# Sending the blank fill of the slot rows earlier in a DMA queue, in longer pieces

## The chip, the cores and the metric

The kernel is one program on one core of a Trainium2 chip. The core has a matrix engine (PE, TensorE), three engines for elementwise work (DVE, ACT, POOL) and SP, which here only issues DMA transfers. Sixteen DMA engines move data between the HBM and the on-chip memory of 128 partitions. The metric is the time of one execution in microseconds on the device, as the median of several runs.

## The reference

A small vision network in two layers over 32 images of 36 tokens (1152 tokens, 128 features), in float32:

```
h = patch_tokens(x)                                # stride-16 patches, four half-patch shifts, layernorm
h = h + transformer(layernorm(h))                  # rotary attention with 8 heads, relu feed-forward, two layernorms
h = h + gelu(layernorm(h) @ tril(W1).T + b1) @ tril(W2).T + b2
h = h + out(groupnorm((softmax(q1 k1) - lam * softmax(q2 k2)) v))     # lam from four vectors of 8 (lambdas)
h = h + moe(h)                                     # attention, then a router: top 2 of 64 experts
# in moe:
pos  = number of earlier picks of the same expert;  keep = pos < 72
buf  = zeros(64, 72, 128);  buf[expert, pos] = token          # 4608 slot rows
y    = gelu(buf @ w1 + b1) @ w2 + b2                          # 64 experts, 512 hidden
out  = x + sum over the two picks of gate * y[expert, pos]
```

Most of the 4608 slots are named by a token; those that are not must hold zeros and an invalid token number.

## The kernel before

All stages up to the router work on four parts of 288 tokens (8 images each), numbered 0 to 3. Each stage name with its part, such as `tok_z:3`, stands in one list per engine (`ORDERS_FOUND`), and the engine executes its list in that order; semaphores join the lists. The start of the lists, as far as it matters here: PE runs `tok_z:0 tok_shift:0 tok_z:1 tok_turn:0 tok_shift:1 tok_z:2 tok_turn:1 tok_shift:2 tok_z:3 tok_turn:2 src_turn:0 tok_shift:3 rope_qk:0`, with filler matmuls (128x128 on the weights, results unused) between some of them; DVE runs `tok_shift:0 tok_norm_a:0 tok_shift:1 tok_norm_a:1 src_norm_a:0 tok_shift:2`; ACT runs `tok_norm_b:1 tok_turn:2 src_norm_b:0` behind POOL's reciprocal root for the same norms. `tok_z` multiplies the patches of a part (waits for `x_in[b]`); `tok_norm_a` takes the moments of a part. In the code of DVE the stage `tok_norm_a:1` begins with `dve.wait_ge(S["lambdas_in"], 16)` and two small products of the lambdas.

SP issues the loads in the order of its code: the patch weights, patches of part 0, columns, constants, patches 1, the rows of biases, patches 2, the other weights (`wT`, blocks 6 and up), patches 3, `lambdas`, router, b1, b2, and the first 11 of the 64 experts' weights (`ring`). All of these go into one queue of SP.

The slot rows (`xslot`, in the HBM, named slot_rows in the profile, 4608 rows of 130 floats) must be filled with a blank row before the tokens are scattered into them: 128 zeros, a token number out of bounds (`NOWHERE`) and one more zero. POOL writes this blank row with two memsets at the very start into the first 130 columns of `hid`, on all 128 partitions, and signals `blank_made`. The fill is one DMA of SP, at the end of its first batch. Two places wait for its end (`blank_sent`): ACT in `net_in:0`, which is the first to write into `hid`, and POOL in `rt_count:0`, ahead of the first scatter (an indirect DMA from `xrow`). After the scatter SP reads the slot rows back for the experts.

Later, POOL clears `mid` and stores it twice into expert_rows, another tensor in the HBM, with one piece per partition. Past the router the kernel walks through the 64 experts, whose weights come through a ring of 11 buffers.

Of the kernel before, what the change touches and what calls it, by code (L numbers as in the profile page):

```python
# [28 lines left out]
D = 128  # L29
# [19 lines left out]
CAP = 2 * (T * 2 // E)  # L49
SLOTS = E * CAP  # L50
ST = SLOTS // D
XW = D + 2
RING = 11
CHUNKS = (2, 6, 8, 8, 8, 8, 8, 8, 8)
# [9 lines left out]
NOWHERE = 1.0e6  # L64
# [208 lines left out]
def build(nc, ins, out):  # L273
# [46 lines left out]
    with ctx:  # L320
        def sb(name, shape, dt=F32):
            return ctx.enter_context(nc.sbuf_tensor(name, shape, dt))

        def sem(name):
            return ctx.enter_context(nc.semaphore(name))
# [47 lines left out]
        third = Share()  # L373
        xrows = third.take([E, XW])
        xe = third.take([NX, CAP])
# [23 lines left out]
        hid = sb("hid", [D, FC, 2, TB])  # L399
# [24 lines left out]
        kept_gate = sb("kept_gate", [TP, NT, 2])  # L424

        xrow = sb("xrow", [TP, 2, TPB, 2, XW])
        blank = hid[:, 0, 0, 0:XW]
        gm = sb("gm", [TP, NT, E])
        put_u = sb("put_u", [CAP, E], U32)

        xslot = nc.dram_tensor("slot_rows", [SLOTS, XW], F32, kind="Internal").ap()
        ytok = nc.dram_tensor("expert_rows", [2 * T, D], F32, kind="Internal").ap()
# [9 lines left out]
        S = {n: sem(n) for n in names}  # L442
# [80 lines left out]
        def tiles(t, b):  # L523
            return t[:, TPB * b:TPB * b + TPB, :]
# [8 lines left out]
        def back_of(b):  # L533

            return ring[0:TP, b, 0:TPB * 2 * D].rearrange("p (n c) -> p n c", n=TPB)
# [4 lines left out]
        @block.sync  # L540
        def _(sp):

            sp.dma_start(wT[:, 0:6, :], ins["weights"][:, 0:6, :]).then_inc(S["patch_weights_in"], 16)
            sp.dma_start(patchT[:, 0, 0:3, :], ins["patches"][:, 0, 0:3, :]).then_inc(S["first_patches_in"], 16)
            sp.dma_start(patchT[:, 0, 3:6, :], ins["patches"][:, 0, 3:6, :]).then_inc(x_in[0], 16)
            sp.dma_start(cols[:, :], ins["cols"]).then_inc(S["cols_in"], 16)
            sp.dma_start(cst[:, :], ins["const"]).then_inc(S["const_in"], 16)
            for b in range(1, NB):
                sp.dma_start(patchT[:, b, :, :], ins["patches"][:, b, :, :]).then_inc(x_in[b], 16)
                if b == 1:  # L550
                    sp.dma_start(rows[:, :, :], ins["rows"].partition_broadcast(TP).rearrange("p (n c) -> p n c", c=D)).then_inc(S["rows_in"], 16)
                if b == 2:
                    sp.dma_start(wT[:, 6:NBLOCKS, :], ins["weights"][:, 6:NBLOCKS, :]).then_inc(S["weights_in"], 16)
            sp.dma_start(lambdas[:, :, :], ins["lambdas"].partition_broadcast(SROWS).rearrange("p (n h) -> p n h", h=H)
                         ).then_inc(S["lambdas_in"], 16)
            sp.dma_start(wr[:, :], ins["router"]).then_inc(S["late_in"], 16)
            sp.dma_start(b1T[:, :, :], ins["b1"]).then_inc(S["late_in"], 16)
            sp.dma_start(b2nat[:, :], ins["b2"]).then_inc(S["late_in"], 16)
            for e in range(RING):
                sp.dma_start(ring[:, e, :], ins["experts"][e]).then_inc(w_here[e], 16)  # L560
            sp.wait_ge(S["blank_made"], 1)
            sp.dma_start(xslot.rearrange("(p n) c -> p n c", p=D), blank[:, :].unsqueeze(1).broadcast_to([D, ST, XW])
                         ).then_inc(S["blank_sent"], 16)
            for b in range(NB - 1):
                sp.wait_ge(slots_sent[b], 16 * 2 * TPB)
            for n in range(2 * TPB):
                sp.wait_ge(last_sent[n], 16)
            for c in range(len(CHUNKS)):
                at = slice(chunk_at[c], chunk_at[c + 1])
                sp.dma_start(xrows[0:CAP, at, :], xslot.rearrange("(s e) c -> s e c", e=E)[:, at, :]).then_inc(rows_here[c], 16)  # L570
            for e in range(RING, E):
                s = e % RING
                sp.wait_ge(S["ys_ready"], e - RING + 1)
                sp.dma_start(ring[:, s, :], ins["experts"][e]).then_inc(w_here[s], 16)

            sp.wait_ge(S["ys_ready"], E)
            for i in range(NY):
                sp.wait_ge(ys_gone[i], 16 * (E // NY))
            for b in range(NB):
                sp.dma_start(back_of(b).rearrange("p n c -> p (n c)"), ytok.rearrange("(b p m) c -> b p (m c)", b=NB, p=TP)[b]  # L580
                             ).then_inc(back_in[b], 16)
            for b in range(NB):
                sp.wait_ge(S["final_ready"], b + 1)
                sp.dma_start(out.rearrange("i s c -> (i s) c").rearrange("(n p) c -> p n c", p=TP)[:, TPB * b:TPB * b + TPB, :],
                             tiles(res, b)).then_inc(S["stored"], 16)
            sp.wait_ge(S["stored"], 16 * NB)
# [3 lines left out]
        def _(pool):  # L590
            st = Steps(pool, S["pool_step"])

            st.step(pool.memset(minus_half[:, :], -0.5))
            st.link(pool.memset(blank[:, :], 0.0))
            pool.memset(blank[:, D:D + 1], NOWHERE).then_inc(S["blank_made"], 1)
            st.step(pool.memset(xTp[:, :, :, :], 0.0))
            pool.memset(run[:, 0, :], 0.0).then_inc(S["run_ready"], 1)
            st.step(pool.memset(ones16[:, :], 1.0))
# [24 lines left out]
            for stage, b in ORDER["pool"]:  # L623
# [52 lines left out]
                if stage == "rt_count":  # L676

                    t = slice(TPB * b, TPB * b + TPB)
# [786 lines left out]
```

## Time and profile before

| | |
|---|---|
| median of 3 runs | 389.16 us (387.92 to 389.21) |
| the profiled execution | 389.98 us, its span 388.3 us |
| PE busy | 347.7 us (90%) |
| DVE, ACT, POOL busy | 233.7, 220.9, 197.4 us |
| DMA | 21239 packets, 50.20 MB |
| the fill, issue to landing | 30.2 us |

PE's busy share is high partly because of the filler matmuls, so it does not say that PE is what sets the end at each place. The DMA engines are full in the first 50 us and again in the expert stage, and nearly idle between them. For a change of the first stage the rows of that stage count.

### The profile page before, as it was taken

To read this page: it belongs to the slowest core of one execution; us is meant where nothing else is said; L and a number is where in the kernel's file an instruction comes from. 1 tells how busy PE (TensorE), PEld (TensorE's weight loads), DVE (VectorE), ACT (ScalarE), POOL (GpSimd) and SP (SyncE) were. 2 spreads that over 40 slices of the span, in tenths; PEclk is the share of its full clock that TensorE was granted. 3 is DMA by queue.
4 is the path that set the end of the run, shared out by engine and by line. 5 is a ranking of instruction groups with operands and counts; after the bars stand their busy time and mean duration, and the time that the engine had idled before them with its cause. 6 is when DMAs were issued, how large, how long until landed. Compare 5 with 4: busy or idle time off the path is not lost.

```text
span 388.3 us, 11371 instructions
## 1 busy us (share of the span) xinstructions
PE 347.7 (90%) x4424; PEld 315.2 (81%) x4424; DVE 233.7 (60%) x615; ACT 220.9 (57%) x640; POOL 197.4 (51%) x312
## 2 busy tenths in 40 slices
PE   8969799999988999997899899499999999999950
PEld 8748687887866889696778788399999999999950
DVE  1446788763489899897868985623335433333314
ACT  1247677777659876677488563103555555555520
POOL 3169687587841112236345767720555555555550
PEclk9999999999999999998999999559999999999995
DMA  7999924000000000000000100037899989999206
GB/s 277 374 391 334 150 28 125 2 2 1 2 3 0 3 3 2 3 2 3 3 3 2 33 9 13 15 95 202 272 320 316 322 308 316 327 324 314 85 9 182
DMA packets 21239, 50.20 MB, mean 129 GB/s; under 512 B 4116, under 2 KB 10340, under 8 KB 21058
## 3 DMA queue, kind: packets, MB, share of 16 engines
q1 hardware_dynamic: 18146, 46.96, 37.9%
q0 software_dynamic: 3040, 2.52, 2.4%
q8 instruction: 36, 0.59, 0.6%
q14 instruction: 17, 0.14, 0.1%
HBM read 43.97 MB, written 7.72 MB: 133 GB/s over the span
## 4 chain that ended last, share of the span: by engine, by line
PE 57%; DVE 12%; ACT 11%; POOL 9%; DMA 6%; issue 4%; SPq 1%; POOLq 0%; DVEq 0%
PE bank L728 34%; PE scores L728 18%; DMA lambdas<-in_lambdas 4%; ACT work L1037 4%; PE bank L803 3%; ACT norm L1037 3%; POOL rstd L613 3%; DVE mx L1266 2%; DVE stats L1203 2%; DVE work L1275 1%; ACT src L1037 1%; PE bank L979 1%; POOL rstd L611 1%; ACT xrow L1037 1%; POOL norm L664 1%
## 5 line engine op out<-in xcount | busy, mean ns | idle before, releaser
L1037 ACT ACTIVATE work<-scores,b1T 128x72 f32<-128x72 f32 x256 | 61.3, 322 | 66.9 <-PE scores L728 66.9
L728 PE MATMUL bank<-ring,work 128*72 128x128 f32 x512 | 97.3, 274 | 0.0
L720 POOL DMA_INDIRECT expert_rows<-work,put_u x64 | 59.9, 935 | 61.7 <-issue 37.7
L728 PE MATMUL scores<-work,ring 128*128 128x72 f32 x512 | 89.0, 258 | 0.2 <-ACT work L1037 0.2
L728 PEld LDWEIGHTS scores<-work,ring 128*128 128x128 f32 x512 | 76.9, 191 | 0.3 <-issue 0.3
L728 PE MATMUL bank<-wT 128*128 128x128 f32 x504 | 72.3, 283 | 2.7 <-ACT work L1037 2.7
L728 PEld LDWEIGHTS bank<-wT 128*128 128x128 f32 x504 | 63.8, 193 | 5.7 <-ACT work L1037 3.1
L1037 ACT ACTIVATE work<-bank 128x288 f32<-128x288 f32 (+3 forms) x136 | 46.7, 376 | 34.4 <-PE bank L728 27.0
L1437 DVE TENSOR_SCALAR work<-bank,work 72x128 f32<-72x128 f32 x64 | 22.2, 347 | 67.5 <-PE bank L728 67.5
L728 PEld LDWEIGHTS bank<-ring,work 128*72 128x72 f32 x512 | 53.8, 145 | 0.2 <-ACT work L1037 0.2
L611 POOL TENSOR_SCALAR rstd<-mv 96x3 f32<-96x3 f32 x32 | 10.1, 315 | 54.8 <-DVE mv L1206 53.6
L613 POOL TENSOR_TENSOR rstd<-rstd,minus_half 96x3 f32<-96x3 f32 x32 | 28.2, 882 | 2.7
L690 POOL DMA_INDIRECT slot_rows<-xrow,flat_u x24 | 24.0, 1001 | 10.5 <-issue 6.1
L1408 DVE TENSOR_SCALAR work<-bank,cols 128x72 f32<-128x72 f32 x64 | 21.7, 341 | 6.8 <-PE bank L979 6.8
L728 PE MATMUL bank<-xTp,wT 128*128 128x288 f32 x80 | 22.9, 416 | 2.3 <-ACT work L1037 1.4
L1037 ACT ACTIVATE work<-work 100x1152 f32<-100x1152 f32 (+1 forms) x20 | 20.2, 1016 | 8.3 <-DVE work L1275 7.0
L1266 DVE TENSOR_REDUCE mx<-scores 100x32 f32<-100x1152 f32 x16 | 21.6, 1351 | 5.0 <-PE scores L728 4.9
L728 PE MATMUL bank<-wT,xTp 128*128 128x128 f32 x192 | 23.8, 277 | 0.4 <-DVE work L1252 0.4
L728 PEld LDWEIGHTS bank<-wT,xTp 128*128 128x128 f32 x192 | 22.5, 192 | 1.4 <-issue 1.2
L1284 DVE TENSOR_REDUCE sm<-work 100x32 f32<-100x1152 f32 x16 | 21.4, 1340 | 3.5 <-ACT work L1037 3.3
L1299 DVE TENSOR_TENSOR work<-work,sm 100x1152 f32<-100x1152 f32 x16 | 21.8, 1360 | 0.6
L1275 DVE TENSOR_TENSOR work<-scores,mx 100x1152 f32<-100x1152 f32 x16 | 21.7, 1358 | 0.6
(159 smaller groups left out, 594.2 us busy)
## 6 DMA issues: line engine op xcount, KB each, us to landing
ring<-in_experts SPq DMA_DIRECT2D x64, 512.0 KB, 5.0
work<-in_patches SPq DMA_DIRECT2D x3, 864.0 KB, 10.6
slot_rows<-hid SPq DMA_DIRECT2D x1, 2340.0 KB, 30.2
work<-slot_rows SPq DMA_DIRECT2D x7, 292.5 KB
wT<-in_weights SPq DMA_DIRECT2D x1, 1664.0 KB, 13.9
expert_rows<-mid POOLq DMA_DIRECT2D x2, 576.0 KB, 5.1
ring<-expert_rows SPq DMA_DIRECT2D x4, 288.0 KB, 4.0
expert_rows<-work,put_u POOLq DMA_INDIRECT x64, 4.4
```

The costliest lines, as they stand in the source:

```text
L611: st.step(pool.tensor_scalar(n, m, -1.0, None, ALU.mult))
L613: st.link(pool.tensor_tensor(r, r, minus_half[0:TP, 0:TPB], ALU.pow))
L690: pool.indirect_dma_start(out=xslot[:, :], out_offset=bass.IndirectOffsetOnAxis(ap=flat_u[:, TPB * b + n, k:k + 1], axis=0), in_=xrow[:, b ...
L720: pool.indirect_dma_start(out=ytok[:, :], out_offset=bass.IndirectOffsetOnAxis(ap=put_u[:, e:e + 1], axis=0), in_=ys[0:CAP, e % NY, :], in ...
L728: return nc.tensor.matmul(o, a, b, start=start, stop=stop)
L1037: return nc.scalar.activation(o, i, f, **kw)
L1266: st.link(v.tensor_reduce(m3, sc, AX_X, ALU.max))
L1275: v.tensor_tensor(e4, sc, m3.unsqueeze(3).broadcast_to([SROWS, QUADS, 2 * PAIRS, SEQ]), ALU.subtract).then_inc(S["exp_in"], 1)
L1284: st.link(v.tensor_reduce(s3, e4, AX_X, ALU.add))
L1299: v.tensor_tensor(to, e4, s3.unsqueeze(3).broadcast_to([SROWS, QUADS, 2 * PAIRS, SEQ]), ALU.mult).then_inc(S["map_scaled" if stage[:3] == ...
L1408: v.tensor_scalar(xe[:, e % NX, :], banks[i][:, 0:CAP], col("L1_ffn_ln2_g"), col("L1_ffn_ln2_b"), ALU.mult, ALU.add).then_inc(S["xe_ready" ...
L1437: v.tensor_scalar(ys[0:CAP, f % NY, :], banks[f % 2][0:CAP, 0:D], xrows[0:CAP, f, D + 1:D + 2], None, ALU.mult).then_inc(S["ys_ready"], 1)
```

## The change

Three edits. The blank source becomes 12 blank rows side by side in `hid` (1560 columns, with `NOWHERE` in 12 of them). The fill writes the same 4608 rows from it, as 384 pieces of 12 rows, where it wrote 4608 pieces of one row. And its issue, with the wait for `blank_made`, moves up in SP's code: behind the second load of `wT`, ahead of the patches of part 3.

```diff
+BLANKS = 12
...
-        blank = hid[:, 0, 0, 0:XW]
+        blank = hid[:, :, :, :].rearrange("p c a t -> p (c a t)")[:, 0:BLANKS * XW].rearrange("p (n c) -> p n c", c=XW)
...
                 if b == 2:
                     sp.dma_start(wT[:, 6:NBLOCKS, :], ins["weights"][:, 6:NBLOCKS, :]).then_inc(S["weights_in"], 16)
+                    sp.wait_ge(S["blank_made"], 1)
+                    sp.dma_start(xslot.rearrange("(p k n) c -> p k (n c)", p=D, n=BLANKS),
+                                 blank.rearrange("p n c -> p (n c)").unsqueeze(1).broadcast_to([D, ST // BLANKS, BLANKS * XW])
+                                 ).then_inc(S["blank_sent"], 16)
...
             for e in range(RING):
                 sp.dma_start(ring[:, e, :], ins["experts"][e]).then_inc(w_here[e], 16)
-            sp.wait_ge(S["blank_made"], 1)
-            sp.dma_start(xslot.rearrange("(p n) c -> p n c", p=D), blank[:, :].unsqueeze(1).broadcast_to([D, ST, XW])
-                         ).then_inc(S["blank_sent"], 16)
...
-            st.link(pool.memset(blank[:, :], 0.0))
-            pool.memset(blank[:, D:D + 1], NOWHERE).then_inc(S["blank_made"], 1)
+            st.link(pool.memset(blank[:, :, :], 0.0))
+            pool.memset(blank[:, :, D], NOWHERE).then_inc(S["blank_made"], 1)
```

SP's instructions from the constants on, before the change (in_patches are the patches of parts 1, 2 and 3, in_b is b1 and then b2, slot_rows<-hid is the fill):

```order
L549 DMA work<-in_patches 128x1728
L551 DMA rows<-in_rows 96x1408
L549 DMA work<-in_patches 128x1728
L553 DMA wT<-in_weights 128x3328
L549 DMA work<-in_patches 128x1728
L554 DMA lambdas<-in_lambdas 100x32
L556 DMA wr<-in_router 128x64
L557 DMA b1T<-in_b 128x256
L558 DMA b2nat<-in_b 64x128
L560 DMA ring<-in_experts 128x1024 x11
L562 DMA slot_rows<-hid 4608x1x130 [waits blank_made]
```

And the same stretch of SP after it:

```order
L550 DMA work<-in_patches 128x1728
L552 DMA rows<-in_rows 96x1408
L550 DMA work<-in_patches 128x1728
L554 DMA wT<-in_weights 128x3328
L556 DMA slot_rows<-hid 384x1x1560 [waits blank_made]
L550 DMA work<-in_patches 128x1728
L559 DMA lambdas<-in_lambdas 100x32
L561 DMA wr<-in_router 128x64
L562 DMA b1T<-in_b 128x256
L563 DMA b2nat<-in_b 64x128
L565 DMA ring<-in_experts 128x1024 x11
```

The fill went past 11 expert loads, b2, b1, the router, the lambdas and the third batch of patches; nothing else on SP changed its place.

The start of POOL's program after the change (minus_half is a constant, hid holds the blank rows):

```order
L595 MEMSET minus_half 128x3
L596 MEMSET hid 128x1560
L597 MEMSET hid 128x12 [waits pool_step]
L598 MEMSET xTp 128x1152
L599 MEMSET run 96x64
L600 MEMSET ones 96x96
L601 MEMSET work 128x2048
L603 CAST before<-cst 96x96 [waits const_in]
```

The order is that of before; the two memsets of hid were 128x130 and 128x1.

## Rows read from the trace of the kernel before

**Rows 1.** The page: the span, and the DMA queue of the instructions.
```profile
span 388.3 us, 11371 instructions
...
q8 instruction: 36, 0.59, 0.6%
```

**Rows 2.** Chain that ended last, 0 to 80 us: start us, us, what.
```profile
6.21 16.35 DMA lambdas<-in_lambdas
...
29.68 7.33 PE bank L728 x52
...
45.23 1.82 issue
```

**Rows 3.** Table of waits: engine, line, releaser, us in total, times, longest.
```profile
DVE lambdas L1221 <- DMA lambdas<-in_lambdas: 4.2, 1, 4.2
```

**Rows 4.** Timeline of PE: start us, us, operation, idle time before it.
```profile
21.31 0.38 PE L728 MATMUL bank<-wT 128*128 128x128 f32 x2
22.38 3.18 PE L728 MATMUL bank<-work,wT 128*128 128x288 f32 x12 [0.69 <-DMA work<-in_patches]
...
26.52 0.90 PE L728 MATMUL bank<-cst,work 128*96 128x128 f32 x6 [0.74 <-DVE work L1235]
```

**Rows 5.** Timeline of SP's issues.
```profile
5.18 0.44 SPq L553 DMA_DIRECT2D wT<-in_weights  x1
5.66 0.51 SPq L549 DMA_DIRECT2D work<-in_patches  x1
...
22.73 1.15 SPq L562 DMA_DIRECT2D slot_rows<-hid  x1
```

**Rows 6.** DMA issues: KB each, median us from issue to landing.
```profile
slot_rows<-hid SPq DMA_DIRECT2D x1, 2340.0 KB, 30.2
...
wT<-in_weights SPq DMA_DIRECT2D x1, 1664.0 KB, 13.9
expert_rows<-mid POOLq DMA_DIRECT2D x2, 576.0 KB, 5.1
```

**Rows 7.** Windows: busy time of each engine, then granted clock, DMA share, GB/s.
```profile
58.50:62.50 4.00, 3.59 (x81) 2.92 (x80) 3.90 (x6) 3.38 (x10) 2.10 (x6) 1.00 0.91 269
22.50:34.50 12.00, 10.11 (x61) 8.23 (x61) 8.83 (x38) 6.30 (x17) 9.23 (x20) 1.00 1.03 410
36.50:49.50 13.00, 10.75 (x191) 9.17 (x190) 10.13 (x17) 8.28 (x23) 9.69 (x20) 1.00 1.22 151
```

**Rows 8.** Timelines of POOL at the start, and of ACT at net_in:0.
```profile
0.83 0.21 POOL L594 MEMSET hid<- 128x130 f32 x1
...
1.13 1.06 POOL L596 MEMSET xTp<- 128x1152 f32 x1
...
8.41 0.26 POOL L601 CAST before<-cst 96x96 bf16<-96x96 f32 x1 [4.27 <-DMA cst<-in_const]
...
64.58 1.66 ACT L1037 ACTIVATE hid<-bank,cols 128x288 f32<-128x288 f32 x4
```

**Rows 9.** PE's timeline and windows at 242 to 262 us, columns as above.
```profile
245.23 0.29 PE L728 MATMUL bank<-oh_both,before 96*96 96x64 bf16 x1 [2.88 <-DVE oh_both L1364]
...
256.79 7.16 PE L728 MATMUL scores<-wT 128*128 128x128 f32 x44
...
243.50:244.00 0.50, 0.00 (x0) 0.00 (x0) 0.50 (x5) 0.48 (x2) 0.23 (x1) 0.92 0.00 0
244.00:244.50 0.50, 0.00 (x0) 0.00 (x0) 0.43 (x3) 0.50 (x1) 0.47 (x1) 0.50 0.17 44
...
260.50:261.00 0.50, 0.50 (x4) 0.50 (x3) 0.00 (x0) 0.00 (x0) 0.00 (x0) 0.52 0.78 200
261.00:261.50 0.50, 0.50 (x7) 0.50 (x6) 0.00 (x0) 0.00 (x0) 0.00 (x0) 1.00 0.72 183
```

**Rows 10.** Timeline of PE's weight loads, at two breaks inside groups of 64.
```profile
47.05 0.17 PEld L728 LDWEIGHTS scores<-work 32*36 32x36 f32 x11 [2.00 <-issue]
...
148.10 0.18 PEld L728 LDWEIGHTS scores<-work 32*36 32x36 f32 x13 [0.30 <-issue]
```

## The prediction

> **What bounds the kernel now.** I read the page first: the span of the profiled execution is 388.3 us [rows 1]. Since the change touches only the first fifty microseconds, I then read the chain that ended last, in order of time. Its first long piece is not computation: from 6.21 us on the chain hangs on one transfer, that of the lambdas, for 16.35 us, and then on PE, in an almost unbroken line of TensorE, ACT and DVE work [rows 2]. The table of waits says who stands there: DVE waits 4.2 us for the lambdas [rows 3]. They are a small transfer (100 x 32 numbers) and nobody needs them before the second attention layer, but the code puts their product ahead of tok_norm_a:1 on DVE, so the whole program passes through them. The second thing that arrives at that moment is the last batch of patches: PE ends the filler ahead of tok_z:3 at 21.69 us, waits, and starts tok_z:3 at 22.38 us [rows 4]. Lambdas and patches land within 0.3 us of each other because they follow one another in one queue.
>
> That queue is SP's. It issues the big weight block at 5.18 us, the last patches at 5.66 us, and the fill of the slot rows only at 22.73 us, behind the eleven expert loads [rows 5]. The weights land 13.9 us after their issue, at about 19.1 us; the fill takes 30.2 us and lands at 52.9 us [rows 6]. Between 22.5 and 34.5 us the sixteen DMA engines move 410 GB/s at a share of 1.03, so they are full; while the fill runs, from 36.5 to 49.5 us, they are full too (1.22) but move only 151 GB/s [rows 7].
>
> **The change part by part.**
>
> The rows of the fill. Before: 4608 pieces of 520 bytes, 2,396,160 bytes, about 15.9 us at 151 GB/s. After: 384 pieces of 6240 bytes. The trace has no store of that kind on SP's queue. From above in speed: loads on this queue run at 410 GB/s [rows 7], which makes 5.8 us. From below: the two stores of expert_rows from mid, 576 KB from 96 partitions, so 6144 bytes a piece [rows 6], ran at 269 GB/s with a share of 0.91 [rows 7]; full engines would make 269 / 0.91 = 296 GB/s of it, which gives 8.1 us. One row has the queue, the other the direction and the piece size, and neither has both, so I take the middle, **7.0 us**, and keep 5.8 and 8.1.
>
> The Trainium skill, "DMA: Bandwidth & Descriptors", Specifications, puts a core's share of the HBM at about 358 GB/s and the fabric at 435 GB/s; an estimate from the page is 6.7 us or 5.5 us for the fill. The trace's 410 GB/s on loads lies above the first figure, so for a core alone I do not hold the kernel to it.
>
> The place of the fill. It now stands in SP's queue ahead of the last patches and the lambdas. Everything of SP behind it goes later by its length: patches 3, lambdas, router, b1, b2, eleven expert loads. Router, b1, b2 and the experts are used in the router and expert stages, long after all of this, so they pay nothing. The weights stand ahead and pay nothing. The last patches hold PE at tok_z:3, the lambdas hold DVE at tok_norm_a:1, and neither has any slack today: both engines were already idle when they came [rows 3, 4]. I looked for work that could fill the longer wait: on DVE everything behind tok_norm_a:1 is in order (src_norm_a:0, tok_shift:2), ACT needs POOL's result of it, and PE needs the patches. So start of both: later by **7.0 us**. SP's wait for blank_made costs nothing: the memset grows from 130 to 1560 columns, by 1152 columns in 1.06 us about 1.4 us instead of 0.21, and ends near 2.5 us, before SP comes there at about 5.7; POOL idles 4.27 us for the constants afterwards [rows 8], which covers the 1.2 us more. Were that cover gone, it would be 1.2 us.
>
> TensorE's clock. PE would now idle from 21.69 to about 29.4 us, 7.7 us. In the trace PE stops at 242.35 us and starts again at 245.23; the granted clock is 0.92 in the half microsecond before 244, and 0.50 after it [rows 9]. So a shorter gap than the new one took the clock to 1.2 GHz. It came back at 261.0 us, 4.2 us after the dense run of 44 matmuls began at 256.79 [rows 9]. tok_z:3 is such a dense run (3.18 us [rows 4]). At half speed for 4.2 us it loses 2.1 us, of which 0.74 us is PE's own idle time ahead of tok_turn:2 [rows 4], where it waits for DVE: **1.4 us** on the path. Floor 0 (no fall). Ceiling: the clock stays low as long as it did after 245.23, 15.8 us, and all of it is PE work: 7.9 less 0.74, or 7.2 us. I take the value near the floor since the work that follows (the 7.33 us run of PE on the chain at 29.68 [rows 2]) is full-width and dense.
>
> The stall inside the fill. In the middle of the 64 score matmuls of rope_scores:1, which wait for nothing among themselves, PE stands still for 1.82 us at 45.23, and that is on the chain [rows 2]; the weight loads show the same hole, 2.00 us, while a hole of the same place in a later group, with DMA idle, is 0.30 us [rows 10]. The page shows a queue for instructions with 36 packets of 0.59 MB in all [rows 1]. My reading, an inference, is that the next instructions came late behind the fill's 520-byte rows. After the change the fill is over by 27 us and the expert loads by about 43 us, and this group runs near 52 us, so the hole should shrink to its size without DMA: 1.82 less 0.30, **1.5 us** won. Bounds 0 and 1.8.
>
> The Trainium skill, "Runtime: NRT & Kernel Launch", Instruction fetch mechanics, says that instructions come in 16 KiB blocks over a DMA queue and that this is mostly hidden. The 36 packets agree with the size. If the hole had another cause, as "mostly hidden" would suggest, the sum would be 1.5 us longer.
>
> The end of the fill. It lands at 52.9 us before, and ACT's first write to hid, which waits for it, starts at 64.58 us [rows 6, 8]; the scatter that also waits for it comes in the router stage. Finishing it earlier wins nothing. Behind 30 us nothing else hangs on a fixed arrival; the chain runs engine to engine, so what is lost at 22 us is not given back.
>
> Sum: 7.0 + 1.4 - 1.5 = **+6.9 us**. The profiled execution has 389.98 us (span 388.3 and 1.7 around it), so 396.9; it lies 0.8 us above the median of 389.16, so the median after is **396.0**.
>
> **The rivals.** (1) The clock stays at half for long after the gap, as between 245 and 261 us: up to 7.2 instead of 1.4 us, 401.9. Against: the work there was small matmuls until 256.79. (2) The fill does not get faster, because its rate is that of scattered writes to memory and not of pieces: 15.9 us instead of 7.0, 405. Against: the stores from mid at 269 GB/s. (3) Not slower: loads use one direction of each engine and the fill the other, so that fill and last patches pass side by side. The decision point is the arrival of the last patches: up to 25.8 us (22.38 and 3.4, of which 1.5 are won back and 1.9 can't be told) it is no measurable change; fully side by side it is 389.2 - 1.5 = 387.7. For it: the share of DMA goes over 1 during the fill. Against: the pieces of one queue are taken in order, as the lambdas behind the patches show. The Trainium skill, "DMA: Bandwidth & Descriptors", Queues, rings and completion order, has it that descriptors are consumed in ring order on each engine but may finish out of order, which leaves both open.
>
> **How the numbers follow.** Forecast 0.80; clock long 0.07; fill slow 0.05; side by side 0.08. The terms' bounds give 5.8 + 0 - 1.8 = 4.0 and 8.1 + 7.2 - 0 = 15.3; all at their worst together is unlikely, so the range goes from 392.5 (just under the low sum, 393.2) to 401.0. What a measurement of this kernel tells from no change is about 0.5%, 1.9 us. Slower 0.92; of the side by side case 0.05 falls within and 0.03 under.
>
> **What would show it.** Last patches: tok_z:3 starts at 28.2 to 30.5 us instead of 22.38, and DVE's wait for the lambdas grows from 4.2 to about 11 us. DMA at some 300 to 400 GB/s throughout 19 to 43 us and idle after. PEclk below 1 for some 6 us after 23 us. The hole in rope_scores:1 under 0.5 us. From the first rope map to the end, the same distances as before. I would be wrong if tok_z:3 starts before 26 us, or if the later stages draw together.

## The result

| | before | changed |
|---|---|---|
| median of 4 runs | 389.19 us (387.92 to 390.31) | 396.22 us (395.78 to 396.61) |
| profiled execution, its span | 389.98, 388.3 us | 395.92, 394.2 us |

The ratio is 1.0182 (95% interval 1.0146 to 1.0218): the change makes the kernel 1.8% slower. Medians in this document are over all executions of a kernel, while ratios and their intervals leave out the executions that took over 1.5% longer than the fastest of the same kernel. The forecast was 396.0 us in a range of 392.5 to 401.0. The path on which the time is lost is the one forecast; several sizes on it are not, and they partly cancel.

The timeline of PE in the changed kernel, which answers to [rows 4]:

```profile
21.05 0.39 PE L730 MATMUL bank<-wT 128*128 128x128 f32 x2
28.20 4.78 PE L730 MATMUL bank<-work,wT 128*128 128x288 f32 x12 [6.76 <-DMA work<-in_patches]
...
33.21 0.90 PE L730 MATMUL bank<-cst,work 128*96 128x128 f32 x6
```

tok_z:3 starts 5.82 us later (28.20 against 22.38), PE idles 6.76 us ahead of it instead of 0.69, and it takes 4.78 us instead of 3.18. tok_turn:2 starts 6.69 us later (33.21 against 26.52).

The waits of its first 60 us, where [rows 3] had 4.2 us:

```profile
DVE lambdas L1223 <- DMA lambdas<-in_lambdas: 11.1, 1, 11.1
...
PE bank L730 <- DMA work<-in_patches: 7.3, 2, 6.8
```

Both waits have grown by about the length of the fill, PE's by 6.1 us and DVE's by 6.9 us. The fill itself, in the table of DMA issues that answers to [rows 6]:

```profile
slot_rows<-hid SPq DMA_DIRECT2D x1, 2340.0 KB, 19.7
...
wT<-in_weights SPq DMA_DIRECT2D x1, 1664.0 KB, 14.1
```

SP issued the fill at 5.55 us and the weights at 5.05, so they landed at 25.3 and 19.2 us: the fill took 6.1 us of the queue. The windows of the changed kernel (busy time of PE, PEld, DVE, ACT, POOL, then granted clock, DMA share, GB/s), which answer to [rows 7, 9]:

```profile
22.00:24.00 2.00, 0.00 (x0) 0.00 (x0) 0.00 (x0) 0.00 (x0) 0.00 (x0) 1.00 1.01 412
24.00:26.00 2.00, 0.00 (x0) 0.00 (x0) 0.00 (x0) 0.00 (x0) 0.00 (x0) 0.66 1.00 394
26.00:28.00 2.00, 0.00 (x0) 0.00 (x0) 0.00 (x0) 0.00 (x0) 0.00 (x0) 0.50 0.80 284
...
31.00:31.50 0.50, 0.50 (x2) 0.36 (x2) 0.44 (x4) 0.00 (x0) 0.42 (x2) 0.53 1.04 418
31.50:32.00 0.50, 0.50 (x3) 0.39 (x3) 0.48 (x2) 0.00 (x0) 0.50 (x1) 1.00 1.07 426
...
164.00:165.00 1.00, 1.00 (x7) 0.83 (x7) 0.14 (x1) 0.00 (x0) 0.00 (x0) 0.80 0.00 0
...
167.00:168.00 1.00, 1.00 (x9) 1.00 (x8) 0.96 (x2) 0.41 (x1) 1.00 (x1) 0.50 0.03 8
168.00:169.00 1.00, 1.00 (x13) 1.00 (x12) 1.00 (x3) 0.95 (x3) 0.55 (x2) 1.00 0.00 0
```

The reader is to see four things. From 22 to 28 us none of the four computing engines does anything. The long pieces go to the HBM at 412 GB/s, as fast as the loads. The clock falls to 1.2 GHz (0.50) from 24.5 us on, while PE waits, and is back at 2.4 GHz in the half microsecond after 31.5. And it falls once more from 164 to 168 us, where nothing of the change is near. The kernel before comes to the same instructions 4 us earlier and has 1.00 there:

```profile
160.00:161.00 1.00, 1.00 (x9) 0.81 (x8) 0.17 (x1) 0.00 (x0) 0.00 (x0) 1.00 0.00 0
```

Going down the two timelines at the same instruction gives the difference in start, before to changed: tok_turn:2 26.52 to 33.21 (+6.7), the first flip of probabilities on PE 50.73 to 55.00 (+4.3), the scores behind it in the second attention 158.16 to 162.13 (+4.0), the group norm's product 177.85 to 183.26 (+5.4), the end of the span +5.9. So the profile loses 6.7 us, wins 2.4 by 55 us, and loses 1.4 again at the dip of the clock. The remaining 0.5 us comes in small steps behind. These 5.9 us are the difference of the two profiled executions. The medians differ by 7.0 us, since the profiled execution of before took 0.8 us more than its median and that of the changed kernel 0.3 us less. Much of the 0.8 us seems to lie in the first stage: three later traces, with the long pieces at the old place, have the same transfers in the same order up to tok_z:3, and start it at 21.34, 21.39 and 21.45 us, not at 22.38. What made the loads land later in the one trace of the kernel before is open. Against these traces the delay of the first stage is 6.8 us at tok_z:3 and 7.4 us at tok_turn:2.

### The profile page after: what moved, and what is told of

The parts are those of the page before. It is cut to its first block, busy times and chain, and to the rows that moved or that the text cites. A ratio compares the mean times of both kernels' runs of the same rounds, so it can differ in the third digit from the quotient of the medians.

```text
span 394.2 us, 11371 instructions
## 1 busy us (share of the span) xinstructions
PE 350.4 (89%) x4424; PEld 317.4 (81%) x4424; DVE 233.6 (59%) x615; ACT 220.8 (56%) x640; POOL 197.6 (50%) x312
## 4 chain that ended last, share of the span: by engine, by line
PE 61%; ACT 10%; DVE 9%; POOL 8%; DMA 7%; issue 3%; SPq 1%; POOLq 0%; DVEq 0%
PE bank L730 38%; PE scores L730 17%; DMA work<-in_patches 6%; ACT work L1039 4%; PE bank L805 3%; ACT norm L1039 3%; POOL rstd L615 2%; ACT src L1039 1%; PE bank L981 1%; DVE stats L1205 1%; POOL rstd L614 1%; PE bank L739 1%; DMA ring<-expert_rows 1%; POOL norm L666 1%; POOL norm L665 1%
## 5 line engine op out<-in xcount | busy, mean ns | idle before, releaser
L613 POOL TENSOR_SCALAR rstd<-mv 96x3 f32<-96x3 f32 x32 | 9.0, 282 | 63.6 <-DVE mv L1208 62.4
L615 POOL TENSOR_TENSOR rstd<-rstd,minus_half 96x3 f32<-96x3 f32 x32 | 28.2, 881 | 2.7
L1410 DVE TENSOR_SCALAR work<-bank,cols 128x72 f32<-128x72 f32 x64 | 21.7, 341 | 7.0 <-PE bank L981 7.0
L1301 DVE TENSOR_TENSOR work<-work,sm 100x1152 f32<-100x1152 f32 x16 | 21.7, 1359 | 0.6
L1277 DVE TENSOR_TENSOR work<-scores,mx 100x1152 f32<-100x1152 f32 x16 | 21.7, 1357 | 0.6
```

What stands on the lines that cost most here:

```text
L615: st.link(pool.tensor_tensor(r, r, minus_half[0:TP, 0:TPB], ALU.pow))
L1277: v.tensor_tensor(e4, sc, m3.unsqueeze(3).broadcast_to([SROWS, QUADS, 2 * PAIRS, SEQ]), ALU.subtract).then_inc(S["exp_in"], 1)
L1301: v.tensor_tensor(to, e4, s3.unsqueeze(3).broadcast_to([SROWS, QUADS, 2 * PAIRS, SEQ]), ALU.mult).then_inc(S["map_scaled" if stage[:3] == ...
L1410: v.tensor_scalar(xe[:, e % NX, :], banks[i][:, 0:CAP], col("L1_ffn_ln2_g"), col("L1_ffn_ln2_b"), ALU.mult, ALU.add).then_inc(S["xe_ready" ...
```

## The experiments

The first four ran on one chip (the kernel before: 389.33 us median there), the other seven on chips where the kernel before takes 402 us. There the first 200 us of the long pieces at the old place run as on the first chip, and from about 216 us on, in the last stages ahead of the router and in the router, holes appear in ACT and PE whose releaser the profile does not name. What makes them is open. They begin far behind the first stage, so for those runs the early part of the timelines carries more than the totals.

**The place alone.** The kernel before, with its fill of 4608 short pieces moved to the new place.

```diff
                 if b == 2:
                     sp.dma_start(wT[:, 6:NBLOCKS, :], ins["weights"][:, 6:NBLOCKS, :]).then_inc(S["weights_in"], 16)
+                    sp.wait_ge(S["blank_made"], 1)
+                    sp.dma_start(xslot.rearrange("(p n) c -> p n c", p=D), blank[:, :].unsqueeze(1).broadcast_to([D, ST, XW])
+                                 ).then_inc(S["blank_sent"], 16)
...
-            sp.wait_ge(S["blank_made"], 1)
-            sp.dma_start(xslot.rearrange("(p n) c -> p n c", p=D), blank[:, :].unsqueeze(1).broadcast_to([D, ST, XW])
-                         ).then_inc(S["blank_sent"], 16)
```

> The fill keeps its 4608 pieces of 520 bytes and only moves ahead of the last patches. If the delay is the length of the fill in the queue, it is 15.9 us here (2.4 MB at the 151 GB/s of the kernel before), so tok_z:3 starts near 38 us; with the 2.4 us that the rest of the first stage won in the changed kernel and the clock about level, the time is 389 + 15.9 - 2.4 = 403 us, at least 401. Rival: the pieces' size does not matter to what waits behind, then it is 396 as with long pieces. Second rival: the loads behind pass it by, then 387 to 390.

Measured: 406.41 us, ratio 1.0454 (1.0382 to 1.0526). PE's timeline:

```profile
39.14 5.97 PE L728 MATMUL bank<-work,wT 128*128 128x288 f32 x12 [17.07 <-DMA work<-in_patches]
```

tok_z:3 starts 16.8 us later than before, close to the 15.9 us worked out, and runs wholly at the low clock (5.97 us against 3.18). Those two differences, 0.9 and 2.8 us less PE's slack of 0.7, make 3.0 of the 3.4 us by which the time lies over the 403 expected. The delay follows the length of the fill in the queue; both rivals fall. SP's timeline shows more:

```profile
5.60 0.65 SPq L555 DMA_DIRECT2D slot_rows<-hid  x1
6.29 19.56 SPq L549 DMA_DIRECT2D work<-in_patches  x1
25.90 1.16 SPq L557 DMA_DIRECT2D lambdas<-in_lambdas  x1
```

SP itself hangs 19.56 us in the issue of the patches behind the 4608 pieces; with 384 pieces that issue takes 0.64 us. So at the new place the long pieces are worth 10 us: 17.1 us are lost without them and 7.0 us with them.

**The long pieces alone**, at the old place behind the expert loads. The cut is shown against the kernel before; the 12 blank rows in hid are those of the change.

```diff
             for e in range(RING):
                 sp.dma_start(ring[:, e, :], ins["experts"][e]).then_inc(w_here[e], 16)
             sp.wait_ge(S["blank_made"], 1)
-            sp.dma_start(xslot.rearrange("(p n) c -> p n c", p=D), blank[:, :].unsqueeze(1).broadcast_to([D, ST, XW])
+            sp.dma_start(xslot.rearrange("(p k n) c -> p k (n c)", p=D, n=BLANKS),
+                         blank.rearrange("p n c -> p (n c)").unsqueeze(1).broadcast_to([D, ST // BLANKS, BLANKS * XW])
                          ).then_inc(S["blank_sent"], 16)
```

> The fill in pieces of 12 rows, at its old place behind the expert loads. It should run from 36 to 42 us and land near 42.5 instead of 52.9. If the hole of 1.8 us inside the score matmuls of rope_scores:1 came from the 520-byte pieces, it is gone and flip:0 starts 2.1 to 2.4 us earlier: 386.8 to 387.1. Rival: the hole has nothing to do with the fill, then 389.2. Nothing in it should move the start of tok_z:3 (22.4 us).

Measured: 387.34 us, ratio 0.9951 (0.9916 to 0.9985). PE's timeline:

```profile
21.45 3.16 PE L730 MATMUL bank<-work,wT 128*128 128x288 f32 x12
...
25.80 0.90 PE L730 MATMUL bank<-cst,work 128*96 128x128 f32 x6 [0.97 <-DVE work L1237]
...
47.59 1.57 PE L805 MATMUL bank<-cst,work 100*128 100x100 f32 x16
```

The first flip starts 3.1 us earlier than in the profile of before, but only 2.4 us of that are the fill's: tok_turn:2 was 0.7 us early already, before the fill had begun, and tok_z:3 0.9 us, which the expectation had not allowed for. Its weight loads on PE, to be read against [rows 10]:

```profile
43.34 0.74 PEld L730 LDWEIGHTS scores<-work 32*36 32x36 f32 x64 [0.15 <-issue]
```

The 64 loads of rope_scores:1 are one row, with no hole. The fetch of instructions gives a likely reason. In the kernel before a block of instructions arrives in the microsecond from 43, while the fill's short pieces are in flight:

```profile
q1 hardware_dynamic: 281, 0.15, 116.6%
q8 instruction: 1, 0.02, 8.9%
```

In the kernel with long pieces that block arrives in the microsecond from 39, 4 us earlier, although the queues are as full:

```profile
q1 hardware_dynamic: 63, 0.39, 98.0%
q8 instruction: 1, 0.02, 7.0%
```

The columns are packets, MB, and the time of the packets as a share of the sixteen engines. Less the 1.1 us by which this execution runs ahead there, the block is about 3 us earlier. The profile does not say for which engine a block is, so that the hole of [rows 2] is this block coming late remains an inference; that the hole goes with the short pieces is shown.

This run also separates the two parts of the change. The changed kernel differs from it by the place alone: 396.22 against 387.34 us, 8.9 us (387.34 is from the first chip, where the kernel before took 389.33 us). The long pieces at the old place win 2.0 us.

**The lambdas ahead of the fill**, the last patches behind it.

```diff
                     sp.dma_start(wT[:, 6:NBLOCKS, :], ins["weights"][:, 6:NBLOCKS, :]).then_inc(S["weights_in"], 16)
+                    sp.dma_start(lambdas[:, :, :], ins["lambdas"].partition_broadcast(SROWS).rearrange("p (n h) -> p n h", h=H)
+                                 ).then_inc(S["lambdas_in"], 16)
                     sp.wait_ge(S["blank_made"], 1)
...
-            sp.dma_start(lambdas[:, :, :], ins["lambdas"].partition_broadcast(SROWS).rearrange("p (n h) -> p n h", h=H)
-                         ).then_inc(S["lambdas_in"], 16)
```

> The changed kernel with the lambdas ahead of the fill; the last patches stay behind it. If the patches alone hold the path, DVE goes on at about 20.5 us, tok_z:3 still starts at 28.2 and ends near 33.2 at the low clock, and the time stays at 396.2 (395.5 to 396.5). Rival: the wait for the lambdas is what costs, then tok_turn:2 comes near 27 us and the time is about 388 to 390.

Measured: 394.97 us, ratio 1.0167 (1.0097 to 1.0237).

```profile
27.84 5.12 PE L730 MATMUL bank<-work,wT 128*128 128x288 f32 x12 [6.64 <-DMA work<-in_patches]
32.80 0.38 PE L730 MATMUL bank<-wT 128*128 128x128 f32 x2
33.02 0.82 PE L730 MATMUL bank<-cst,work 128*96 128x128 f32 x6
```

DVE is free from 18.85 us, and tok_turn:2 still starts at 33.0. The patches and the slow clock by themselves cost the whole delay. The median lies 1.2 us under that of the changed kernel, but four executions between 392.86 and 396.89 us do not settle such a difference. The profiled one is the fastest of them. It is 3.1 us shorter than that of the changed kernel, 0.4 us of it by 40 us; the rest comes at two dips of the clock of the changed kernel that it does not have, from 164 and from 188 us (the kernel before has the second one, from 182 us, too).

**The last patches ahead of the fill**, the lambdas behind it.

```diff
                     sp.dma_start(wT[:, 6:NBLOCKS, :], ins["weights"][:, 6:NBLOCKS, :]).then_inc(S["weights_in"], 16)
-                    sp.wait_ge(S["blank_made"], 1)
-                    sp.dma_start(xslot.rearrange("(p k n) c -> p k (n c)", p=D, n=BLANKS),
-                                 blank.rearrange("p n c -> p (n c)").unsqueeze(1).broadcast_to([D, ST // BLANKS, BLANKS * XW])
-                                 ).then_inc(S["blank_sent"], 16)
+            sp.wait_ge(S["blank_made"], 1)
+            sp.dma_start(xslot.rearrange("(p k n) c -> p k (n c)", p=D, n=BLANKS),
+                         blank.rearrange("p n c -> p (n c)").unsqueeze(1).broadcast_to([D, ST // BLANKS, BLANKS * XW])
+                         ).then_inc(S["blank_sent"], 16)
             sp.dma_start(lambdas[:, :, :], ins["lambdas"].partition_broadcast(SROWS).rearrange("p (n h) -> p n h", h=H)
                          ).then_inc(S["lambdas_in"], 16)
```

> The changed kernel with the last patches ahead of the fill; the lambdas alone stay behind it. If the lambdas by themselves hold the path as long as the patches do, DVE waits to 29 us, tok_turn:2 starts at 33 and the time is 396. The clock may fall once more, since PE then idles from 25.8 to 33 us, which would add up to 0.8. Rival: the patches are what costs, then 388 to 390.

Measured: 396.40 us, ratio 1.0202 (1.0123 to 1.0281).

```profile
21.88 3.12 PE L730 MATMUL bank<-work,wT 128*128 128x288 f32 x12
...
33.08 1.59 PE L730 MATMUL bank<-cst,work 128*96 128x128 f32 x6 [7.85 <-DVE work L1237]
```

tok_z:3 runs at once, and tok_turn:2 still starts at 33.1, since DVE waits for the lambdas (10.4 us). It is 1.59 us long instead of 0.90 because now it is the one that meets the low clock. The low clock then leaves PE 0.75 us behind the changed kernel at src_turn:0 (36.95 against 36.20 us), as the expectation allowed. So either of the two transfers alone costs the full delay, and moving one of them back wins nothing in the stage where it waits.

**The clock, in two runs**: 27 filler matmuls instead of one ahead of tok_z:3, with the lambdas as in the changed kernel, and with the lambdas ahead of the fill.

```diff
-    tok_z:0=5 tok_shift:0=4 tok_shift:1=1 tok_turn:1=2 tok_z:3=1 tok_turn:2=1 src_turn:0=3 rope_qk:0=4 tok_turn:3=2
+    tok_z:0=5 tok_shift:0=4 tok_shift:1=1 tok_turn:1=2 tok_z:3=27 tok_turn:2=1 src_turn:0=3 rope_qk:0=4 tok_turn:3=2
```

> The changed kernel with 27 filler matmuls instead of 1 ahead of tok_z:3, so that PE works through most of its wait (0.25 us each, to about 27.7 us) and the clock stays at 2.4 GHz. If the low clock after the wait costs the path nothing because DVE, held by the lambdas until 29.3 us, is as late as PE, tok_z:3 takes 3.2 instead of 4.8 us, tok_turn:2 still starts at 33.2 us and the early stages stand where they stood. The prediction's term says otherwise: 1.4 us won, tok_turn:2 near 32. The later dip of the clock at 164 us may come or not, 1.4 us; the total 394.5 to 396.5.

> The lambdas ahead of the fill and the 27 filler matmuls together. With the lambdas alone moved, PE's tok_z:3 at the low clock (5.1 us) holds tok_turn:2 at 33.0 us. If the clock is what costs there, both together start it at about 31.2 us, 1.8 us earlier, and the time is 1.8 us under that of the kernel with the lambdas moved, 393.2. Rival: something else holds tok_turn:2 and it stays at 33.

Measured: 407.76 us, ratio 1.0197 (1.0151 to 1.0244), and 404.80 us, ratio 1.0118 (1.0093 to 1.0144). The filler with the lambdas behind the fill:

```profile
28.51 3.18 PE L730 MATMUL bank<-work,wT 128*128 128x288 f32 x12 [1.18 <-DMA work<-in_patches]
31.52 0.38 PE L730 MATMUL bank<-wT 128*128 128x128 f32 x2
34.11 0.90 PE L730 MATMUL bank<-cst,work 128*96 128x128 f32 x6 [2.20 <-DVE work L1237]
```

and with the lambdas ahead:

```profile
28.21 3.18 PE L730 MATMUL bank<-work,wT 128*128 128x288 f32 x12 [0.40 <-DMA work<-in_patches]
31.22 0.38 PE L730 MATMUL bank<-wT 128*128 128x128 f32 x2
31.44 0.82 PE L730 MATMUL bank<-cst,work 128*96 128x128 f32 x6
```

In both, tok_z:3 takes 3.18 us again, so the 1.6 us (1.9 us with the lambdas ahead) were the clock's. In the first they win nothing: PE merely waits 2.20 us for DVE, and tok_turn:2 starts at 34.11 us, 0.9 us later than expected, since in this execution the lambdas came 0.9 us later (30.18 us). In the second, tok_turn:2 starts at 31.44 instead of 33.02, 1.6 us won of the 1.8 expected. The low clock costs the changed kernel nothing by itself; it costs 1.6 us only once the lambdas are out of the way.

**Long traffic of long pieces**: the long pieces at the old place, and three more such stores to a tensor that nothing reads (its declaration is left out here, as are the two waits for `blank_sent`, which now count all four stores).

```diff
+            for i in range(3):
+                sp.dma_start(spare.rearrange("(i p k n) c -> i p k (n c)", i=4, p=D, n=BLANKS)[i],
+                             blank.rearrange("p n c -> p (n c)").unsqueeze(1).broadcast_to([D, ST // BLANKS, BLANKS * XW])
+                             ).then_inc(S["blank_sent"], 16)
```

> The long pieces at the old place, and behind them three more stores of the same size and piece length into another tensor of the HBM, which nothing reads, so that the DMA engines are full with long pieces until about 60 us. ACT's write to hid waits for all four. If the hole in rope_scores:1 needs short pieces, it is absent here too (weight loads idle under 0.5 us inside the group) and the time stays near 387.3, or a little over for net_in:0. Rival: any full queue delays it, then the hole of about 2 us is back at 43 us and the time is 389 or more.

Measured: 405.90 us, ratio 1.0106 (1.0046 to 1.0166). Its profiled execution was the longest of its four (409.68 us), so only its first 65 us are read here. The stores run at the loads' rate:

```profile
42.00:58.00 16.00, 13.95 (x303) 12.32 (x305) 12.77 (x26) 12.57 (x35) 13.29 (x20) 1.00 1.02 412
```

And the weight loads:

```profile
43.30 0.74 PEld L735 LDWEIGHTS scores<-work 32*36 32x36 f32 x64 [0.16 <-issue]
...
53.38 0.63 PEld L735 LDWEIGHTS bank<-wT,xTp 128*128 128x128 f32 x5 [1.64 <-issue]
61.66 0.60 PEld L735 LDWEIGHTS bank<-work 128*32 128x32 f32 x33 [3.46 <-issue]
```

Both expectations were half right. The hole in rope_scores:1 stays away, but two others open at 53.4 and 61.7 us, inside groups that wait for nothing. The next two blocks of instructions arrive in the microseconds from 50 and from 59:

```profile
q1 hardware_dynamic: 65, 0.41, 101.1%
q8 instruction: 1, 0.02, 6.8%
...
q0 software_dynamic: 68, 0.36, 95.0%
q8 instruction: 1, 0.02, 6.6%
```

With long pieces alone, where the queues are idle, they arrive from 44 and 52 us. At the second block it is POOL's own stores (queue 0) that fill the engines. So blocks come late behind long pieces too, and short pieces are not needed for a hole, as far as one execution can show it. What long pieces seem to have done for the kernel is to end the traffic before the next block was wanted.

**Better orders.** Three runs beside each other: long pieces alone again; with the lambdas moved up behind the columns; and with, on top of that, the last patches ahead of the big weight block and the fill behind it (this last one also ran a first time in the set before).

```diff
             sp.dma_start(cols[:, :], ins["cols"]).then_inc(S["cols_in"], 16)
+            sp.dma_start(lambdas[:, :, :], ins["lambdas"].partition_broadcast(SROWS).rearrange("p (n h) -> p n h", h=H)
+                         ).then_inc(S["lambdas_in"], 16)
...
-                if b == 2:
-                    sp.dma_start(wT[:, 6:NBLOCKS, :], ins["weights"][:, 6:NBLOCKS, :]).then_inc(S["weights_in"], 16)
...
-            sp.dma_start(lambdas[:, :, :], ins["lambdas"].partition_broadcast(SROWS).rearrange("p (n h) -> p n h", h=H)
-                         ).then_inc(S["lambdas_in"], 16)
+            sp.dma_start(wT[:, 6:NBLOCKS, :], ins["weights"][:, 6:NBLOCKS, :]).then_inc(S["weights_in"], 16)
+            sp.wait_ge(S["blank_made"], 1)
+            sp.dma_start(xslot.rearrange("(p k n) c -> p k (n c)", p=D, n=BLANKS),
+                         blank.rearrange("p n c -> p (n c)").unsqueeze(1).broadcast_to([D, ST // BLANKS, BLANKS * XW])
+                         ).then_inc(S["blank_sent"], 16)
             sp.dma_start(wr[:, :], ins["router"]).then_inc(S["late_in"], 16)
```

> The kernel with long pieces at the old place, once more, beside the next two on one chip. Theory: 0.5 to 0.8% faster than the kernel before (2.4 to 3 us), since the hole in rope_scores:1 is gone. Rival: the 0.5% seen first was chance, then it is the same within 0.3%.

> Long pieces at the old place and the lambdas moved up, behind the columns. DVE then works on tok_norm_a:1 from about 20 us. If the lambdas were 1 us of the path (PE waited 0.97 us for DVE ahead of tok_turn:2), tok_turn:2 starts near 24.9 us instead of 25.8 and the time is 0.7 to 1 us under that of long pieces alone. Rival: it is not, PE's own work or the patches hold it, then the same.

> Long pieces, in another order: the lambdas behind the columns, the last patches ahead of the big weight block, then the weights, the fill, router, b1, b2, experts. Nothing that the first stages wait for stands behind the fill. tok_z:3 should start right behind its filler at 21.7 us, and tok_turn:2 at about 25.2 us instead of the 25.8 of the kernel with long pieces alone: 386.5 us, 0.6 to 1 us under that. Rival: the weights, now last, hold rope_qk:0 (they would have to come after 29 us), then it is slower than long pieces alone.

> Long pieces, the lambdas behind the columns, the last patches ahead of the big weight block and the fill behind it, once more beside the others. If the patches of part 3 still set the path with the lambdas early, it is up to 0.7 us under the kernel with the lambdas moved; if PE reaches tok_z:3 no earlier than they land in any case, it is the same. It should be 0.8 to 1.2% faster than the kernel before.

Measured: long pieces alone 399.00 us, ratio 0.9911 (0.9873 to 0.9949); with the lambdas up 401.72 us, 0.9990 (0.9952 to 1.0028); the full new order 401.04 us, 0.9990 (0.9951 to 1.0029), and again 399.91 us, 0.9991 (0.9951 to 1.0032). Long pieces alone beat the kernel before on the first chip. On this one the sign is the same, but it is less sure than the interval says: the executions of either kernel scatter over 10 us, and the medians of all of them are 399.00 and 401.99 us. The other orders do not clear the noise of this chip. PE's timeline with the lambdas up:

```profile
21.95 0.38 PE L730 MATMUL bank<-wT 128*128 128x128 f32 x2
22.31 3.18 PE L730 MATMUL bank<-work,wT 128*128 128x288 f32 x12
25.32 0.38 PE L730 MATMUL bank<-wT 128*128 128x128 f32 x2
25.54 0.88 PE L730 MATMUL bank<-cst,work 128*96 128x128 f32 x6
```

PE no longer waits for DVE, but its filler ahead of tok_z:3 starts at 21.95 us where it starts at 21.10 with long pieces alone on the same chip, presumably since every load behind the lambdas comes later, the constants and the patches of part 1 among them. tok_turn:2 is at 25.54 against 25.68: of the 0.94 us that PE idled there, 0.14 is left as gain. With the full new order tok_z:3 starts at 22.45 and 22.21 us where 21.7 was expected, and tok_turn:2 at 25.81 and 25.56 where 25.2 was. So all three expectations of a further gain were wrong, the 0.8 to 1.2% under the kernel before among them. Nor does the first stage explain that the kernel with the lambdas up has a median 2.7 us above that of long pieces alone: its profiled execution is 0.8 us ahead at 255 us and falls behind only from 259 us on, in the router stage, at a hole of 2.58 us that has no named releaser.

## Why the prediction was right, and where it was not

**The path.** Right: last patches and lambdas stand behind the fill and both come later by about its length. The place alone (+16.8 us at tok_z:3 for a fill of 15.9) and the two runs with one of them moved back (33.0 and 33.1 us at tok_turn:2) show it. With long pieces the place costs 8.9 us by the medians (7.0 + 1.4 = 8.4 were put down, but the 8.9 hold the dip of the clock at 164 us, which was not foreseen), and the pieces win 2.0 us (1.5 were put down).

**The length of the fill, 7.0 us.** Too high for the fill itself: it took 6.1 us of the queue, near the 5.8 us of the fast bound, with long pieces at 412 GB/s. The delay of the patches is less sure. It is 5.82 us against the one profile of the kernel before, and 6.8 us against the long pieces at the old place, close to the 7.0; behind the fill the queue moved only 284 GB/s from 26 to 28 us, and why it did is open. The row of the stores from mid (296 GB/s when scaled to full engines [rows 7]), on which I leaned for the middle, is of a short transfer from POOL's queue, presumably with its start and end in the window. The 358 GB/s that the Trainium skill, "DMA: Bandwidth & Descriptors", Specifications, gives as a core's share of the HBM is passed here by stores as well as loads, on this one core. Against the profile of before the lambdas came 6.68 us later, 0.86 more than the patches ahead of them; what delays them that much more I did not isolate.

**The clock, 1.4 us.** It fell and came back as described, after 3.3 us of tok_z:3 and not 4.2, and tok_z:3 lost 1.6 us by it, 0.9 more than PE's 0.74 us of slack. But as a term added to the fill's length it was wrong: that sum took both branches to be held equally long, which leaves the slack of PE against DVE as it was, while DVE was held for 6.68 us by the lambdas and PE for 5.82 by the patches. The two branches met at 33.2 us, PE's 5.82 + 1.60 - 0.74 = 6.68 and DVE's 6.68. Filler matmuls alone won nothing at tok_turn:2; with the lambdas ahead they won 1.6 us. Fill and clock together were put at 8.4 us; at tok_turn:2 they measured 6.7 us against the profile of before, or 7.4 us against the long pieces at the old place.

**The hole, 1.5 us won.** Right in kind, too small: by the first flip 2.4 us were won. Of these, 0.3 us came ahead of the hole, where PE had waited 0.42 us for DVE at 41.50 us, and 2.1 us at the hole itself. PE's hole went to 0, not to the 0.30 us of the row I compared it with, and DVE had been idle 1.97 us behind it. That the fetch of instructions is the cause was an inference; the block that comes about 3 us earlier bears it out and does not prove it. By the Trainium skill, "Runtime: NRT & Kernel Launch", Instruction fetch mechanics, the fetch is mostly hidden. The traces agree for idle queues; with full ones the block from 39 us cost nothing, and the later ones of the run with three more stores stand beside holes of up to 3.46 us.

**Not given back.** The statement that nothing behind 30 us gives the time back held, but the reverse was missed: a new dip of the clock at 164 us costs 1.4 us in the profiled execution; why it comes there is open. By the steps, 6.9 us was 7.0 + 1.4 - 1.5, and the profiles give 6.7 - 2.4 + 1.4 + 0.2 = 5.9. The median's 396.22 lies so near to 396.0 partly by chance: the medians are 7.0 us apart, 1.1 more than the profiled executions, and an overrated clock, an underrated hole and a dip that nobody foresaw about cancel.

**The rivals.** The clock staying low for long did not happen (7 us after 24.5). The fill as slow as before fell with its 6.1 us. Side by side fell with the arrival of the patches at 28.2 us.

## What to carry to other kernels

A transfer that nobody waits for belongs behind all that somebody waits for in its queue; its price when it stands ahead is its bytes over the rate of the queue, paid once on each branch that waits, and branches that wait in parallel do not add. Before adding a clock penalty to a wait, follow the other branch to the point where they meet. Long pieces are worth having wherever the transfer stands: here they won 2 us at the harmless place and 10 us at the harmful one. And one profiled execution is one execution: before reading a difference of 1 us out of two traces, compare each with the median of its set.

## What the runs showed of the hardware

Pieces of 520 bytes from the on-chip memory to the HBM moved at 151 GB/s, pieces of 6240 bytes at 412 GB/s in the same queue. Behind 4608 short pieces SP's own issue of the next load took 19.56 us; behind 384 long ones it took 0.64 us.

The granted clock of the same instructions was not the same in every kernel. In the changed kernel it was 0.50 between about 164 and 168 us, where the kernel before ran the same instructions at 1.00, 4 us earlier; it is not seen there with the lambdas ahead of the fill, nor with the last patches ahead. The dip from 188 us of the changed kernel stands in the profile of before too, 6 us earlier, and is absent with the lambdas ahead. Each is read from one execution. The first of them moved the total by about 1.4 us, more than some of the edits compared here.

Blocks of 16 KiB of instructions (0.59 MB in 36 packets on their queue) came in the microseconds from 43, 50 and 59 us when the data queues were full, against 39, 44 and 52 us with long pieces alone, and in the same executions PE stood for 1.6 to 3.5 us inside groups of matmuls that waited for nothing else.
